# Gain and shift of an output norm, moved from the end of the kernel into its expert loop

## The reference

```python
probs = softmax(xf @ Wr + br)
vals, idx = top_k(probs, 2)
w = vals / vals.sum(-1)                       # two weights per token
for ei in range(16):
    h = silu(xf @ W1[ei]) * (xf @ W3[ei])     # 128 -> 512
    y = h @ W2[ei]                            # 512 -> 128
    y = (y - mean(y)) * rsqrt(var(y) + 1e-5) * gamma[ei] + beta[ei]
    out = out + combine[:, ei:ei+1] * y       # combine holds w at the two chosen experts
x = x + s * silu(out)                         # s: the recurrent branch
```

## Time and profile before

| what | us |
|---|---|
| median of three runs | 1211.29 (1208.75 to 1212.32) |
| the profiled execution | 1212.35, of which the span of the trace is 1210.6 |
| PE busy | 1129.3 (93% of the span) |
| DVE busy | 915.2 (76%) |
| ACT busy | 805.2 (67%) |

### The profile page before, as it was taken

How to read it: one execution, slowest core, us unless ns; L and a number is a source line. 1 busy time by engine, 2 the same in 40 slices (tenths; PEclk the granted TensorE clock), 3 DMA queues, 4 the chain that set the end, 5 groups by cost and what they waited for, 6 DMA issues and landing times.

```text
span 1210.6 us, 19401 instructions
## 1 busy us (share of the span) xinstructions
PE 1129.3 (93%) x6417; PEld 471.0 (39%) x6417; DVE 915.2 (76%) x1403; ACT 805.2 (67%) x1490; POOL 346.8 (29%) x860
## 2 busy tenths in 40 slices
PE   5979999999999999999999999999999677899995
PEld 2412222222222222222222345444444353899994
DVE  3589999999999999999999754333334879466665
ACT  2668898888888888888888854333333444255551
POOL 0376653243222342222322110000000011356651
PEclk9779999999999999999999999999999869899995
DMA  3313321032100322102011222100000011467743
GB/s 113 138 28 81 89 72 55 31 94 55 47 29 28 87 60 49 33 32 67 29 31 36 71 80 126 35 18 18 17 17 1 0 36 51 150 210 238 236 130 115
DMA packets 65253, 85.81 MB, mean 71 GB/s; under 512 B 28562, under 2 KB 39834, under 8 KB 64898
## 3 DMA queue, kind: packets, MB, share of 16 engines
q1 hardware_dynamic: 54306, 69.95, 18.3%
q0 software_dynamic: 10208, 13.45, 4.8%
q10 hardware_dynamic: 646, 1.23, 0.3%
HBM read 58.79 MB, written 25.76 MB: 70 GB/s over the span
## 4 chain that ended last, share of the span: by engine, by line
PE 40%; issue 33%; POOL 19%; DVE 7%; ACT 1%; DMA 1%; POOLq 0%; SPq 0%; ACTq 0%; DVEq 0%
PE PS L1691 9%; PE PS L1701 9%; PE PS L1869 7%; POOL neg_m L635 6%; POOL big L449 4%; PE PS L1879 3%; POOL big L467 2%; PE PS L1466 1%; PE PS L1815 1%; DVE mx L1052 1%; POOL m_cols L640 1%; POOL m_cols L642 1%; POOL m_rest L641 1%; POOL m_rest L643 1%; POOL m_cols L644 1%
## 5 line engine op out<-in xcount | busy, mean ns | idle before, releaser
L1052 DVE TENSOR_REDUCE mx<-PS 128x1 f32<-128x1024 f32 x512 | 593.9, 1213 | 21.4 <-PE PS L1538 10.3
L1553 PE MATMUL PS<-big 59*128 59x512 bf16 x1024 | 295.1, 387 | 7.3 <-ACT xnT L812 1.6
L1538 PE MATMUL PS<-big 56*128 56x512 bf16 x1024 | 202.0, 385 | 15.5 <-DVE mx L1052 8.5
L812 ACT ACTIVATE ctx_sb<-PS 128x512 f32<-128x512 f32 x344 | 187.8, 604 | 23.2 <-PE PS L1553 23.2
L812 ACT ACTIVATE xn<-PS 128x512 f32<-128x512 f32 x340 | 185.7, 604 | 26.2 <-PE PS L1553 26.2
L812 ACT ACTIVATE xnT<-PS 128x512 f32<-128x512 f32 x340 | 185.6, 605 | 21.6 <-PE PS L1553 21.6
L1553 PEld LDWEIGHTS PS<-big 59*128 59x128 bf16 x1024 | 72.7, 93 | 323.2 <-ACT ctx_sb L812 98.2
L1182 DVE TENSOR_TENSOR ctx_sb<-big,PS 128x512 f32<-128x512 f32 x128 | 87.9, 687 | 132.2 <-PE PS L1701 78.2
L864 ACT ACTIVATE big<-PS,col_sb 128x512 f32<-128x512 f32 x128 | 87.9, 687 | 133.0 <-PE PS L1691 119.9
L635 POOL TENSOR_SCALAR neg_m<-mx 128x1 f32<-128x1 f32 x256 | 68.6, 287 | 371.6 <-DVE mx L1052 371.6
L1691 PE MATMUL PS<-big,w_bufs 128*128 128x512 f32 x256 | 133.5, 604 | 0.1
(11 more groups left out here) (263 smaller groups left out, 1119.7 us busy)
## 6 DMA issues: line engine op xcount, KB each, us to landing
big<-in_w_in SPq DMA_DIRECT2D x47, 512.0 KB
o_dram<-o_sum SPq DMA_DIRECT2D x64, 256.0 KB, 2.3
big<-parts_dram POOLq DMA_DIRECT2D x42, 128.0 KB, 4.6
w_bufs<-in_w SPq DMA_DIRECT2D x16, 256.0 KB, 2.6
big<-in_w_out SPq DMA_DIRECT2D x2, 2048.0 KB, 11.6
w_bufs<-o_dram SPq DMA_DIRECT2D x3, 1024.0 KB, 5.0
big<-parts_dram SPq DMA_DIRECT2D x62, 48.0 KB
big<-m_dram SPq DMA_DIRECT2D x128, 3.0 KB
```

What stands on the lines that cost most here:

```text
L812: nc.scalar.activation(probs[i % SLOTS][:, r, :], PS[:, SB + n % SLOTS, :], ACT.Exp, scale=DH ** -0.5).then_inc(exp_done, 1)
L1052: v.tensor_reduce(mx[:, b % 2, 2 * u + half:2 * u + half + 1], PS[:, MB + 2 * half:MB + 2 * half + 2, :].rearrange("p b n -> p (b n)"), AX ...
L1538: mm = pe.matmul(PS[:, MB + 2 * half + k, :], q_all[rows_of, h, t * P:(t + 1) * P], k_all[rows_of, h, half * CH:(half + 1) * CH], start=Tr ...
L1553: pe.matmul(PS[:, SB + n % SLOTS, :], k_all[rows_of, h, at:at + P], q_all[rows_of, h, qc * CH:(qc + 1) * CH], start=True, stop=True).then_ ...
```

## The change

- Gain and shift of all 16 experts are laid out as rows, `gains[0]` and `gains[1]`, and loaded once into every partition (`gain_rows`, `shift_rows`, 1 MB each in the SBUF), early in the first layer's mixture of experts. DVE picks the row of a tile's expert by a register: `expert(n)` reads the expert's number from `te_i`.
- `take_output` no longer copies. The statistics read PSUM, and one instruction subtracts the mean, multiplies with the expert's gain and writes the ring. `finish_outputs` multiplies with the inverse root and adds the expert's shift.
- The groups are ten of four tiles, three of two and one of one. The first nine go as before (root on ACT, finished three iterations after the last tile). The last eleven tiles (a group of four, three of two, one of one) get their inverse root from DVE alone, by three Newton steps, and are finished one iteration after their last tile.
- At the end the weights of the two experts are applied per tile of tokens: ACT scales `y1`, DVE multiplies `y2` and adds. SP loads `y1` and ACT's queue loads `y2`. The products on PE and ACT's copies of the shift are gone, and the chunks overlap.

```diff
+ROOTED = (NT - 11) // 4
-GROUPS = [*(range(i, i + 4) for i in range(0, NT - 3, 4)), range(NT - 3, NT - 1), range(NT - 1, NT)]
+GROUPS = [*(range(i, i + 4) for i in range(0, NT - 7, 4)), *(range(i, i + 2) for i in range(NT - 7, NT - 2, 2)),
+          range(NT - 1, NT)]
...
+            sp.wait_ge(ctx_ready, C)
+            sp.dma_start(gain_rows, gains[0].partition_broadcast(P)).then_inc(gains_in, 16)
+            sp.dma_start(shift_rows, gains[1].partition_broadcast(P)).then_inc(gains_in, 16)
...
-            for c in range(C):
-                for k, y in enumerate((y1, y2)):
-                    at = k * N + c * CH
-                    sp.dma_start(y[:, c * TC:(c + 1) * TC, :], ...
+            load_rows(sp, 0, y1)
...
-                    if n == min(group[-1] + 2, NT - 1):
+                    if n == group[-1] + 2:
                         roots(i)
...
+            load_rows(act, 1, y2)
+            def scale_rows(c):
+                act.wait_ge(rows_back[c], 16 * 2)
+                for t in range(c * TC, (c + 1) * TC):
+                    nc.scalar.activation(y1[:, t, :], y1[:, t, :], ACT.Copy, scale=wgt[:, 0, t:t + 1])\
+                        .then_inc(rows_scaled, 1)
...
-            def weigh_experts():
...
+            def expert(n):
+                return dve.value_load(te_i[0:1, bass.ds(n, 1)], min_val=0, max_val=E1 - 1)
...
             def take_output(n):
                 r = n % RING
+                e = expert(n)
                 dve.wait_ge(yt_mm, n + 1)
...
-                v.tensor_copy(y_ring[:, r, :], PS[:, YB + n % 2, 0:P]).then_inc(yt_dve, 1)
-                dve.wait_ge(yt_dve, n + 1)
-                ch.step(v.bn_stats(y_st[:, r, :], y_ring[:, r, :]))
+                y = PS[:, YB + n % 2, 0:P]
+                ch.step(v.bn_stats(y_st[:, r, :], y))
                 ch.step(v.bn_aggr(y_mom[:, r, :], y_st[:, r, :]))
+                v.scalar_tensor_tensor(y_ring[:, r, :], y, y_mom[:, r, 0:1], gain_rows[:, bass.ds(e * P, P)],
+                                       ALU.subtract, ALU.mult).then_inc(yt_dve, 1)
...
             def finish_outputs(i):
-                dve.wait_ge(y_std, i + 1)
                 at = slice(GROUPS[i][0] % RING, GROUPS[i][-1] % RING + 1)
-                ch.step(v.reciprocal(y_rstd[:, at], y_rstd[:, at]))
+                if i < ROOTED:
+                    dve.wait_ge(y_std, i + 1)
+                    ch.step(v.reciprocal(y_rstd[:, at], y_rstd[:, at]))
+                else:
+                    dve.wait_ge(y_var, i + 1)
+                    ch.step(inverse_roots(y_rstd[:, at], rms[:, at].bitcast(U32), rs[:, at]))
+                dve.wait_ge(yt_dve, GROUPS[i][-1] + 1)
                 for n in GROUPS[i]:
                     r = n % RING
-                    last = v.tensor_scalar(y_ring[:, r, :], y_ring[:, r, :], y_mom[:, r, 0:1], y_rstd[:, r:r + 1],
-                                           ALU.subtract, ALU.mult)
+                    e = expert(n)
+                    last = v.scalar_tensor_tensor(y_ring[:, r, :], y_ring[:, r, :], y_rstd[:, r:r + 1],
+                                                  shift_rows[:, bass.ds(e * P, P)], ALU.mult, ALU.add)
...
-                    if n == group[-1] + 3 and i < len(GROUPS) - 2:
+                    if n == group[-1] + (3 if i < ROOTED else 1):
                         finish_outputs(i)
...
+            def mix_rows(c):
                 dve.wait_ge(rows_back[c], 16 * 2)
+                for t in range(c * TC, (c + 1) * TC):
+                    dve.wait_ge(rows_scaled, t + 1)
+                    last = v.scalar_tensor_tensor(y2[:, t, :], y2[:, t, :], wgt[:, 1, t:t + 1], y1[:, t, :],
+                                                  ALU.mult, ALU.add)
...
+            def add_experts(c):
                 dve.wait_ge(silu1, c + 1)
+                ch.step(v.tensor_tensor(chunk(y2, c), chunk(y2, c), chunk(s1, c), ALU.mult))
+                v.tensor_tensor(chunk(x_sb, c), chunk(x_sb, c), chunk(y2, c), ALU.add).then_inc(done, 1)
+            mix_rows(0)
+            for c in range(C):
+                if c + 1 < C:
+                    mix_rows(c + 1)
+                add_experts(c)
```

More of the change, by code:

```diff
@@ L364, in build @@
         pos_set = sem("pos_set")
-        hot_w_set = sem("hot_w_set")
+        gains_in = sem("gains_in")
+        rows_scaled = sem("rows_scaled")
         te_set = sem("te_set")
@@ L468, in load_chunk, with load_rows @@
                     .then_inc(chunk_in, 16)
-        def chunk_shift(c):
-            return big[:, c * CH:(c + 1) * CH].rearrange("p (t d) -> p t d", t=TC)
+        def load_rows(eng, k, y):
+            for c in range(C):
+                at = k * N + c * CH
+                eng.dma_start(y[:, c * TC:(c + 1) * TC, :],
+                              yt_dram[at:at + CH, :].rearrange("(t p) d -> p t d", p=P)).then_inc(rows_back[c], 16)
         @block.sync
@@ L967, in _ @@
                     copy_slots(n + 3)
-                for i, group in enumerate(GROUPS):
-                    if n == min(group[-1] + 2, NT - 1):
+                for i, group in enumerate(GROUPS[:ROOTED]):
+                    if n == group[-1] + 2:
                         roots(i)
-            for c in range(C):
[L972 to L979, removed]
+            act.wait_ge(s_gated, C)
+            act.wait_ge(y_out, 16 * NT)
+            load_rows(act, 1, y2)
[4 more added lines that the diff above has]
+                        .then_inc(rows_scaled, 1)
+            scale_rows(0)
+            for c in range(C):
+                if c + 1 < C:
+                    scale_rows(c + 1)
                 act.wait_ge(mixed, c + 1)
-                nc.scalar.activation(y1[:, c * TC:(c + 1) * TC, :], y1[:, c * TC:(c + 1) * TC, :], ACT.Silu)\
+                nc.scalar.activation(y2[:, c * TC:(c + 1) * TC, :], y2[:, c * TC:(c + 1) * TC, :], ACT.Silu)\
                     .then_inc(silu1, 1)
@@ L1422, in _ @@
                 if n == 3 + C:
-                    weigh_experts()
+                    dve.wait_ge(second_dve, SECOND_DVE.n("Y"))
+                    dve.nop().then_inc(s_gated, C)
                 for i, group in enumerate(GROUPS):
-                    if n == group[-1] + 3 and i < len(GROUPS) - 2:
+                    if n == group[-1] + (3 if i < ROOTED else 1):
                         finish_outputs(i)
             take_output(NT - 1)
-            for i in range(len(GROUPS) - 2, len(GROUPS)):
-                finish_outputs(i)
@@ L1432, in _ @@
-            for c in range(C):
[L1433 to L1437, removed]
-                ch.did(v.tensor_tensor(chunk(y1, c), chunk(y1, c), g1, ALU.mult))
-                ch.did(v.tensor_tensor(chunk(y2, c), chunk(y2, c), g2, ALU.mult))
-                ch.settle()
-                ch.step(v.tensor_tensor(chunk(y1, c), chunk(y1, c), chunk(y2, c), ALU.add))
-                v.tensor_tensor(chunk(y1, c), chunk(y1, c), chunk_shift(c), ALU.add).then_inc(mixed, 1)
@@ L1443, in _ @@
-            for c in range(C):
-                dve.wait_ge(silu1, c + 1)
-                ch.step(v.tensor_tensor(chunk(y1, c), chunk(y1, c), chunk(s1, c), ALU.mult))
-                v.tensor_tensor(chunk(x_sb, c), chunk(x_sb, c), chunk(y1, c), ALU.add).then_inc(done, 1)
+            finish_outputs(len(GROUPS) - 1)
+            def mix_rows(c):
+                dve.wait_ge(rows_back[c], 16 * 2)
+                for t in range(c * TC, (c + 1) * TC):
+                    dve.wait_ge(rows_scaled, t + 1)
+                    last = v.scalar_tensor_tensor(y2[:, t, :], y2[:, t, :], wgt[:, 1, t:t + 1], y1[:, t, :],
+                                                  ALU.mult, ALU.add)
+                    if t < (c + 1) * TC - 1:
+                        ch.did(last)
+                ch.settle()
+                last.then_inc(mixed, 1)
```

44 lines of the change are left out of this document (7 added, 37 removed).

## The result

The changed kernel takes 1228.32 us (median of four runs, 1226.15 to 1231.27); the kernel before took 1210.02 in the same runs (four, 1208.67 to 1212.32). The ratio is 1.015, with a 95% interval of 1.0125 to 1.0174. The forecast was 1228. The profiled execution took 1228.56, its span is 1226.7, so the two traces are 16.1 us apart, as their spans are.

A forecast was written before the change was run, and what follows sets the result against it. PE was taken to bound the loop, DVE the stretch from tile 39. Loop +10.4, last stretch +16.2, row loads -5.5 and mixing -4.9 summed to +16.2: 1227.5 against the median, stated as 1228, range 1213 to 1238.

The forecast's parts named there:

- the sum: Whole execution: +10.4 + 16.2 - 5.5 - 4.9 = +16.2 us, against the profiled execution of 1212.35.
- Price of a load: DVE's register read of the expert's number: 0.735 us each, built from SP's durations, gaps and 0.07 for handing over.
- One behind the other in the finish, hidden in `take_output`: DVE's reads: serial behind the reciprocal in `finish_outputs`, hidden behind the waiting multiply in `take_output`.
- A group's stall: Expert loop: each finished group of four starts PE's layer 1.27 us late; groups 0 to 7 cost +10.4.
- The slack: Expert loop, before tile 38's hidden layer: 1.15 us left at the tightest place, once per group of four.
- The last stretch: From tile 39's multiply to the last normalized tile, DVE the bound: 40.1 us against 23.9, +16.2.
- The end: After the last normalized tile: row loads -5.5 us, load to mixing left at 3.8, mixing -4.9.
- The products on PE at no gain: End: removing PE's products gains nothing, for their results waited for the rows.
- That loads cost nothing: Rival on DVE's reads: the sequencer runs ahead, no group stalls, -5, 1206 us; chance 0.11.
- the 1242 that followed from it: Whole-kernel estimate if the skill's floor of about 600 ns per `tensor_load` held: 1.05 us per load, 1242 us.
- PE's clock: Rival in the loop's new stalls: one tile per stall at 1.2 instead of 2.4 GHz, +14, 1241 us; chance 0.07.
- The row that I argued from the earlier trace: PE's clock: PE busy 1.39 of 4 us still had full clock, so stalls of 1.3 should not lower it.

The follow-up runs named there:

- Newton roots alone: Kernel before with only the pairs for the last tiles and Newton-step roots of the last five groups, no expert read: 1211.64 us, ratio 1.0001.
- the kernel with two reads: Changed kernel with two register loads instead of one per tile in the finishing of a group: 1272.59 us, ratio 1.0504.

## Why the prediction was right

The mechanism was right: the reads stand in DVE's queue, the loop and the last stretch pay, and the end gives some back. That the sum met the traces to 0.1 is luck in part. The loop's stalls were sized 2.6 too small and the end's gain 1.5 too small, and the last stretch and the mixing missed by less than 1 each; an execution that came 1.3 sooner to tile 7 made up the rest.

**Price of a load (0.735).** Measured by the pitch of the shifts, 0.754. That is closer than its parts: the register operations on DVE take 190 and 69 ns, where I took SP's 152 and 42, the load 301 instead of 268, so 0.583 for the four instead of 0.48; the gaps are 0.17 and not the 0.255 that I had added. The row that I read as DVE's own address operation, 46 ns, was not its price: the address here takes 69. The two misses cancelled, so how close the price came is luck.

**One behind the other in the finish, hidden in `take_output`.** Shown both ways: with the 47 reads of `take_output` alone the loop takes 89.26, against 89.25 with none; doubling the others moves the pitch from 0.754 to 1.38. In the last stretch the reads of `take_output` cost 2.3, about what the sum has there (0.15 per taken output and the last tile's load); reading them early gave 1.3 back.
The Trainium skill, Perfetto Trace Analysis, section "Sequencer-only Instruction (DRAIN, etc)", has the next instruction fetched only when such a one is done. The pitch of 0.754, and of 1.38 with two reads, agrees for DVE. The Trainium skill, DMA: Bandwidth & Descriptors, section "Latency and other measured facts", gives about 600 ns as the floor of a `tensor_load`; 301 here does not agree, and the 1242 that followed from it did not come.

**A group's stall (1.27).** The step held, the size was small: from tile 7 to 39 the eight groups cost 102.29 - 89.33 = 12.96, 1.62 each (the first 1.83, the others 1.57 to 1.61). Of the 0.3 that are missing in most of them, 0.07 is the finish (5.14 instead of 5.07), 0.10 the way from the end of the multiply to PE's start (0.15, I had 0.05), 0.07 the late layer itself (2.02 instead of 1.95), and 0.17 is how I read the slack. The chain dates the hidden layer at 1147.93; its part of a layer is 1.79 long, but the layer in the timeline of PE is 1.95 and starts at 1147.76 in the same execution (the first of these rows is the layer that the multiply of tile 35 follows):

```profile
1142.19 1.95 PE L1869 MATMUL PS<-big 128*128 128x128 f32 x16
...
1147.76 1.95 PE L1869 MATMUL PS<-big 128*128 128x128 f32 x16
```

The chain counts only what nothing else covers. The slack was 0.98, not 1.15. Against these the multiply of tile 35 comes 0.07 sooner after PE's layer (1.13 after 1152.34, before 1.20). In all 1.61. In the sum +11.7 stands against +10.4 and not +13, because this execution is already 1.3 ahead at tile 7 (1063.94 against 1065.22); why is not settled.

**The last stretch (40.1).** Measured 39.7. The eleven small instructions of a Newton chain are 0.197 apart instead of 0.215, 2.13 in all and not 2.35; the loads, 0.02 longer each, took some of that back.

**The end (-5.5, 0, -4.9).** Measured -7.0, +0.8, -5.1. From the last normalized tile to the row loads it is 2.6 and not 4.1: the way from the last scatter's issue to the load, 3.77 before, is 2.29 here, and 2.29 to 2.31 in all ten experiments. I took the one row that was there, and it is the exception: even Newton roots alone, with the end of before, has 2.31. Why the trace of before has 3.77 is not shown. Part of it came back, since the way from load to first mixing, 4.6, includes ACT's scaling of four tiles.

**The products on PE at no gain.** Right. In the trace of before the four products that the first mixing needs were done 4.2 us ahead of it, and those of the later chunks 1.9 us or more. With Newton roots alone the rows are loaded sooner, and the four are still 4.3 ahead.

**The rivals.** That loads cost nothing would have given 1206; without reads it is 1205.69, so the price of that case was right and its condition was not met. PE's clock did not fall in the stalls of 1.4 (in busy times of the changed kernel, granted clock in the third column from the end):

```profile
1130.00:1160.00 30.00, 25.92 (x229) 25.30 (x228) 17.16 (x52) 13.17 (x25) 17.84 (x19) 1.00 0.65 210
1160.00:1190.00 30.00, 24.15 (x213) 23.57 (x212) 19.42 (x70) 9.29 (x18) 16.16 (x17) 1.00 0.41 131
```

It is 1.00 in the other stretches of the loop too, from 1040 on. In the last stretch a stall of 3.17 ahead of the layer at 1181.18 left it there; after a later one of 4.22 it fell at 1197, within the last output layer (1.46 instead of 1.06). With stalls three times as long in each group it fell in most of them, as the kernel with two reads shows. The row that I argued from the earlier trace rows was weak ground: from 960 to 964, right behind it, PE is busy for 0.00 and the granted clock is 0.61.

## What to carry to other kernels

Before putting a read of a number into an engine's queue, look at what stands behind it on that queue: the same read was free in the loop behind a multiply that waited anyway, and cost 0.53 behind a reciprocal, with a multiply for PE queued behind four of them. If the number is needed twice, read it once and keep it; that one edit turned 1.5% slower into 0.27% faster (0.12 to 0.42). When an instruction waits for several semaphores, check what the profile names as the end of its wait: the row that named PE's products had waited for rows from a DMA. And measure a slack between the rows of the timeline: a chain of waits shows only the uncovered part of a step.

## What the hardware showed beside this

- The same register read costs different amounts on different engines: load, operations, assertion and address are 268, 152, 18 and 42 ns on SP, and 301, 190, 23 and 69 ns on DVE.
- PE's clock stayed at 2.4 GHz through stalls of 1.4 us in every group, and dropped to 1.2 GHz after one of 4.17 (granted clock 0.57 over that stretch). Between these it went both ways: with two reads it fell at a stall of 3.59 (0.50 from 1090 to 1096) and not at one of 3.68 (1.00 from 1172 to 1190).
- An operand addressed from a register that was loaded long ago still cost DVE 0.13 us where the instruction waits for its predecessor (0.16 idle against 0.03).
